# Leaf rows summed on VectorE instead of GpSimd, with another order of calls on every engine

## What is computed

```python
h = patches @ W.T + b                                        # tok
h = h + attn(layernorm(h))                                   # attn: x*res_scale + (u * (relu(qk/sqrt_s)^2 @ v)) @ o_w.T
logits = x @ W_in.T + b_in                                   # ffn, x = layernorm(h), 8 trees x 255 nodes
moves = logits > 0                                           # walk down: 7 decisions in each tree
out = (silu(logits) * visited) @ W_out.T                     # only the 8 nodes on the path are kept
h = h + out
```

## Time and profile before

| | |
|---|---|
| median of 3 runs | 2026.34 us (2025.54 to 2026.86) |
| profiled execution, own time | 2028.2 us |
| its span, first to last instruction | 2026.4 us |
| mean granted TensorE clock | 0.991 |
| PE busy | 1973.2 us, 97% |
| DVE busy | 1702.8 us, 84% |
| ACT busy | 1397.2 us, 69% |
| POOL busy | 1001.6 us, 49% |

### The profile page before, as it was taken

The page is one execution under the profiler, slowest core; times in us unless marked ns, Lnnn a source line. Parts: engine busy times, 40 slices in busy tenths (PEclk is TensorE's granted clock), DMA queues, the critical chain, the costliest instruction groups (busy, mean ns, idle before and its releaser), DMA issues. The chain is left out here.

```text
span 2026.4 us, 41146 instructions
## 1 busy us (share of the span) xinstructions
PE 1973.2 (97%) x12488; PEld 1858.1 (92%) x12488; DVE 1702.8 (84%) x4210; ACT 1397.2 (69%) x3085; POOL 1001.6 (49%) x1001
## 2 busy tenths in 40 slices
PE   6799999999999999999999999999999999999997
PEld 5689999999999999999999999999999999999986
DVE  5598888898888898888898888898888898888875
ACT  5467776677776676776676776676776776776764
POOL 2675445545445545445545545545545545545544
PEclk8999999999999999999999999999999999999999
DMA  4423223223222223223233223232223233222222
GB/s 131 108 75 93 76 77 82 79 72 90 77 75 81 78 76 87 74 77 80 75 83 84 75 76 82 73 86 83 75 75 81 74 87 83 75 75 79 61 68 80
DMA packets 81999, 163.12 MB, mean 80 GB/s; under 512 B 17102, under 2 KB 48048, under 8 KB 81968
## 3 DMA queue, kind: packets, MB, share of 16 engines
q0 software_dynamic: 40960, 103.02, 19.3%
q1 hardware_dynamic: 41008, 59.71, 10.3%
HBM read 148.76 MB, written 13.90 MB: 80 GB/s over the span
## 5 line engine op out<-in xcount | busy, mean ns | idle before, releaser
L483 POOL DMA_INDIRECT leaf_rows<-leaf_table,leaf_at x512 | 582.2, 1137 | 156.0 <-issue 156.0
L861 DVE TENSOR_TENSOR hid_lo<-hid,hid_hi 128x392 fp32r<-128x392 f32 (+1 forms) x256 | 255.3, 997 | 77.3 <-ACT hid_hi L551 77.2
L1168 PE MATMUL out_acc<-hid_hi,outw_lo 128*128 128x392 f32 x768 | 300.3, 391 | 0.2 <-DVE hid_lo L861 0.2
L456 POOL TENSOR_TENSOR inv_root<-to_root,minus_half 98x8 f32<-98x8 f32 x64 | 95.7, 1495 | 412.7 <-DVE to_root L911 266.1
L1168 PE MATMUL hid_ps<-ffn_x,in_lo 128*128 128x392 f32 x768 | 272.1, 354 | 1.8 <-ACT hid L706 0.7
L1170 PE MATMUL out_acc<-hid_hi,outw_hi 128*128 128x392 f32 x768 | 263.4, 343 | 0.0
L1169 PE MATMUL hid_ps<-ffn_x,in_hi 128*128 128x392 f32 x768 | 262.8, 342 | 0.0
L1169 PE MATMUL out_acc<-hid_lo,outw_hi 128*128 128x392 f32 x768 | 262.2, 341 | 0.0
L1170 PE MATMUL hid_ps<-ffn_x,in_hi 128*128 128x392 f32 x768 | 261.4, 340 | 0.0
L496 POOL TENSOR_TENSOR row_sum<-leaf_rows,row_sum 98x1024 f32<-98x1024 f32 x96 | 221.3, 2305 | 40.3 <-ACT leaf_rows L743 34.6
L482 POOL TENSOR_TENSOR held<-minus_half 98x1 f32<-98x1 f32 x128 | 35.7, 279 | 373.6 <-ACT v_full L637 199.6
(11 more groups left out here) (142 smaller groups left out, 5854.6 us busy)
## 6 DMA issues: line engine op xcount, KB each, us to landing
x_raw<-x SPq DMA_DIRECT2D x192, 196.0 KB, 2.4
out<-out_stage SPq DMA_DIRECT2D x32, 392.0 KB
leaf_rows<-leaf_table,leaf_at POOLq DMA_INDIRECT x512
leaf_table<-leaf_rows SPq DMA_DIRECT2D x4, 256.5 KB, 4.2
out_stage<-in_w SPq DMA_DIRECT2D x4, 256.0 KB
tok_major<-tok_w SPq DMA_DIRECT2D x3, 256.0 KB, 4.3
late_raw<-out_w SPq DMA_DIRECT2D x6, 128.0 KB
u<-uv_w SPq DMA_DIRECT2D x1, 576.0 KB, 4.2
```

Source lines behind the costliest of these rows:

```text
L483: pool.indirect_dma_start(row_slot(s, g), None, table, bass.IndirectOffsetOnAxis(ap=leaf_at[:, s, g:g + 1], axis=0), element_offset=s * P ...
L861: dve.tensor_tensor(out, src, hi.bitcast(F32), ALU.subtract).then_inc(done, 1)
L1168: pe.matmul(out, w[1], x_parts[0], start=start, stop=False)
```

## The change

`scale_rows` on ACT is left for the first tree only. For trees 1 to 3 a new `sum_rows` on DVE does scaling and adding in one instruction for each group of 98 tokens: row times activation (a scalar for each partition, read from `leaf_act`) plus sum. POOL's `sum_rows` goes. The counts that the fetches wait for follow. In addition every engine's table of calls is written in another order, and the cut between two trips lies elsewhere.

The hunks below are, in this order, the count of sums, POOL's `sum_rows`, ACT's `scale_rows`, DVE's new `sum_rows`, and the first calls of DVE's table.

```diff
-SUMS = GATHERED - 1
+SUMS = (GATHERED - 1) * GROUPS
...
-            def sum_rows(i, s):
...
-                pool.tensor_tensor(row_sum[:, :, :], leaf_rows[0:HALF, at:at + GROUPS, ROW_IN:ROW], row_sum[:, :, :],
-                                   ALU.add).then_inc(rows_summed, 1)
...
-            def scale_rows(i, s):
+            def scale_rows(i):
...
+            def sum_rows(i, s):
+
+                if i is None:
+                    return
+                dve.wait_ge(leaf_active, GATHERED * i + s + 1)
+                if s == 1:
+                    dve.wait_ge(rows_scaled, GROUPS * (i + 1))
+                for g in range(GROUPS):
+                    if s > 1:
+                        dve.wait_ge(rows_summed, SUMS * i + GROUPS * (s - 2) + g + 1)
+                    dve.scalar_tensor_tensor(row_sum[:, g], row_slot(s, g)[:, ROW_IN:ROW], leaf_act[:, s, g:g + 1],
+                                             row_sum[:, g], ALU.mult, ALU.add).then_inc(rows_summed, 1)
...
             def body(p, i, n, nx):
+                leaf_dots(p, 3)
+                x_low(n, 5)
+                sum_rows(p, 2)
+                sum_rows(p, 3)
+                hid_low(p, 6)
+                ffn_x_low(i, 0)
+                ffn_x_low(i, 1)
+                mask(p, 7)
                 norm_stats(n, 0, 0)
                 norm_stats(n, 0, 1)
                 norm_moments(n, 0)
                 decisions(i, 0)
```

More of the change, by code:

```diff
@@ L1080, in body @@
                 decisions(i, 0)
+                decisions(i, 1)
+                mask(i, 0)
                 hid_low(p, 7)
-                mask(i, 0)
-                decisions(i, 1)
                 hid_low(i, 0)
@@ L1091, in body @@
                 xn_low(n, 1)
+                mask(i, 2)
                 residual(n, 0)
@@ L1131, in body @@
                 mix_low(n, 3)
-                leaf_dots(i, 2)
+                hid_low(i, 5)
+                x_low(nx, 2)
                 mask(i, 6)
@@ L1135, in body @@
                 update_h(n, 1)
-                decisions(i, 7)
-                x_low(nx, 2)
+                leaf_dots(i, 2)
                 norm_stats(n, 1, 0)
                 norm_stats(n, 1, 1)
+                x_low(nx, 3)
                 norm_moments(n, 1)
-                x_low(nx, 3)
-                leaf_dots(i, 3)
+                decisions(i, 7)
                 x_low(nx, 4)
-                hid_low(i, 5)
-                x_low(nx, 5)
-                hid_low(i, 6)
-                ffn_x_low(n, 0)
-                ffn_x_low(n, 1)
-                mask(i, 7)
             dve.sem_inc(out_stored, 16)
@@ L1419, in body @@
             def body(p, i, n, nx):
+                turn_xn(i, 0)
+                turn_xn(i, 1)
+                tree_visits(p, 2)
+                tree_logits(p, 4, 0)
+                turn_normed(i, 0)
+                tree_out(p, 0, 0)
+                tree_out(p, 0, 1)
+                tree_visits(p, 3)
+                turn_normed(i, 1)
+                tree_out(p, 1, 0)
+                find_leaf(p, 2)
+                make_base(i)
+                tree_out(p, 1, 1)
+                if first(i):
+                    turn_rows()
+                make_v(i, 0)
+                tree_logits(p, 4, 1)
+                make_v(i, 1)
+                find_leaf(p, 3)
+                make_v(i, 2)
+                tree_logits(p, 5, 0)
+                make_v(i, 3)
+                tree_out(p, 2, 0)
+                tree_visits(p, 4)
+                tree_out(p, 2, 1)
                 make_u(i, 0)
[L1421 removed]
+                tree_out(p, 3, 0)
+                make_u(i, 1)
                 tree_logits(p, 5, 1)
                 scores(i, 0)
[L1424 removed]
+                scores(i, 1)
+                tree_out(p, 3, 1)
                 tree_logits(p, 6, 0)
[L1426 removed]
+                make_u(i, 2)
+                make_u(i, 3)
+                tree_logits(p, 6, 1)
+                mix(i, 0)
                 tree_visits(p, 5)
[L1428 to L1432 removed]
                 mix(i, 1)
                 mix(i, 2)
+                tree_out(p, 4, 0)
                 mix(i, 3)
                 tree_visits(p, 6)
[L1437 to L1438 removed]
+                tree_out(p, 4, 1)
                 project_o(i, 0, range(0, 3))
```

218 lines of the change are left out of this document (85 added, 133 removed).

## The result

The changed kernel takes 2035.21 us in the median of 6 runs (2032.7 to 2038.73), the kernel before 2026.44 us in 6 runs. The ratio is 1.0046 with a 95% interval of 1.0033 to 1.0059: slower by 0.46%, 8.8 us. The forecast was 2038 us, in a range of 2020 to 2048.

The account below looks back on a forecast made before the run. PE's own work was taken to bound the loop, with small waits tied to DVE. Loop +12.5, start +2.0 and end -2.7 us sum to +11.8 us on the median 2026.34, giving 2038 us, range 2020 to 2048.

Parts of the forecast that it names:

- tied DVE chain: DVE from `update_h(n, 1)` to the visit: 17.34 us behind `embed`; PE waits 0.80 us a period instead of 0.29.
- 29 periods: Loop between the first and 30th `add_rows`: +0.51 - 0.08 = +0.43 us a period, +12.5 us over 29.
- The new instruction: DVE's scale-and-add, 98 x 256: 0.345 us like a dot plus 0.05 to 0.06 for the scalar, taken as 0.40 us.
- not slower, about 2026: Rival: the new DVE instruction costs 0.345 us like a dot, so the period stays the old one; chance 0.16.
- The relief of DVE from POOL's addition: Long `hid_lo` in the tied stretch, held by POOL's addition, shortens; 2.0 us come back to DVE there.
- "wrong" sign: Profile sign against the forecast: a period of 60.9 us or less, or a PE wait elsewhere, above all at `turn_xn` or `mix`.
- The step saved on PE: `find_leaf(i, 1)` directly ahead of `turn_xn` saves one late second matmul, 0.08 us a period.
- The start: First unit: `norm_roots(0, 0)` starts at 24.7, 3.3 us later, and the unit hangs on it; +2 us, bounds -1 and +5.
- The end: Last unit: fetches and dot freed from POOL's addition 3.2 us earlier, eight sums added, `tree_out` of tree 5 earlier; -2.7 us.
- Faster, about 2015: Rival: DVE reaches the visit in time, chain 0.8 us shorter, both waits and one step go; chance 0.17.
- Slower still: Rival, about 2057 us: a new DVE instruction costs 0.48 us, 18.6 us more; chance 0.08.
- the relief fails: Rival, about 2096 us: a gather, not POOL's addition, held `hid_low`, which still takes 2.98 us; 58 us more; chance 0.02.

Follow-up runs that it names:

- experiment with a constant: Changed kernel, its 12 new DVE instructions using the constant 1.0 instead of the activation read for each partition; 2024.51 us, ratio 0.9995.
- experiment with the short addition: Kernel before, POOL's three additions cut to one column of each group; 2019.97 us, ratio 0.9971.
- version with the split sums: Changed kernel, tree 1's fetch no longer waiting for the next unit's first v, the last two of tree 3's four sums behind `decisions(i, 1)`; 2018.58 us.
- versions that move the sums of tree 3: Changed kernel, tree 3's four sums moved behind `decisions(i, 1)`: 2050.23 us; also without tree 1's fetch wait: 2041.28; only two sums moved, without that wait: 2018.58.
- Taking the hold away: Changed kernel, POOL's first gather of tree 1 no longer waiting for the next unit's first v; 2026.18 us, ratio 1.000.
- a start 5 us earlier: Version with the split sums, plus the first unit's last x piece split ahead of the v and u weights and `norm_roots(0, 0)` earlier on POOL; 2018.12 us.
- old tables with the sums replaced: Kernel before with its own tables, sums on DVE: tree 1 ahead of `gate(n, 0)`, tree 3 behind `decisions(i, 1)`, POOL's additions gone; 2034.73 us, ratio 1.0044.

## Why the prediction was right, step by step

The size and the sign were right, the mechanism in part. The period is longer by the tied DVE chain that the prediction named, and by a wait that it didn't have, and the second is the larger part: against the 0.29 us of before, the two places of the chain have 0.14 us more, and `mix` has 0.30. Of the three terms, the loop's came out near its size with this exchange inside, the end's was near, and the start's had the wrong sign. Start and end are read from one profiled execution of each kernel.

| term | predicted | measured (spans) |
|---|---|---|
| 29 periods | +12.5 us | +11.3 us |
| up to the first `add_rows` | +2 us | -1.9 us |
| from the 30th to the end | -2.7 us | -1.9 us |
| sum | +11.8 us | +7.5 us (medians +8.8) |

**The new instruction.** 0.40 us predicted, 0.396 measured, and the two parts that it was put together from (0.345 for the dot's shape, 0.05 to 0.06 for the scalar) came out as 0.336 and 0.060. The Trainium skill, page "VectorE: DVE Perf Modes", section on the TRN2 errata, has 58 + N cycles, an estimate of 0.33 us, and nothing for the scalar. The experiment with a constant agrees with it (0.336); with the activation the measurement decides. That was the step on which the sign hung: at 0.336 the kernel ties with the one before (2024.5 us), as the rival "not slower, about 2026" said. (The "about 2024" that the prediction has for 0.33 us is a slip: by its own terms, 8 x 0.07 us less in the chain, it comes to about 2022.)

**The relief of DVE from POOL's addition.** Right: no long `hid_lo`, 763 ns in the mean for 997, and the experiment with the short addition shows that it was the addition. The longest `hid_lo` of the loop is 2.99 us before, 0.97 after and 0.98 with the short addition. The Trainium skill, page "SBUF — State Buffer", section "Who interferes with whom", has an exclusive lock between such instructions; the traces agree. The experiment also showed what the prediction had only as an argument, that the hold cost the old loop next to nothing (60.93 us with and without).

**The tied chain.** Predicted 17.34 us from `embed` to the visit, measured 16.98. The steps between were 12.54 and came out as 12.26, and `mask` cost 0.95 instead of 1.03 (which was near its duration, 1.04, and not a distance between starts). The sums were 3.17 for 3.20; the rest is that `norm_stats` costs 1.34 us where the next instruction doesn't use its result (1055.02 to 1056.36), against the 1.46 that I took from a row where it does, and a few hundredths each in `ffn_x_low`, `hid_low` and the dots. So PE waits 0.43 us at the two places, not 0.80. This is the term that was mis-sized. Both waits are there, but of the second only 0.05 us depend on the chain: 0.13 to 0.16 us stay at the visit in every kernel in which `turn_h` doesn't wait for `ffn_x_low`, for there `norm_stats` waits for `turn_h` itself, and from `turn_h` to the visit it is 4.22 to 4.27 us by way of DVE. The prediction also took the old wait ahead of `turn_h(n, 0)`, 0.15 us, for one of the same kind. It wasn't. `ffn_x_low` had ended 0.98 us earlier, and ACT's `copy_h`, which writes what `turn_h` transposes, 0.05 us earlier, at 1060.18:

```profile
1059.11 1.07 ACT L574 ACTIVATE hT<-hid_ps,col 128x392 f32<-128x392 f32 x2
```

With ACT's new table `copy_h` ends 0.49 us ahead of `turn_h`. So "PE hardly waits for it, so I cost that at nothing" left out half of the old loop's waits: 0.15 us a period, 4 us in all, which the version with the split sums has back.

**The wait that I didn't see.** The "wrong" sign that I named for the profile, a wait at `mix`, is there, with 0.30 us; the other place named, `turn_xn`, has one in the versions that move the sums of tree 3. The new tables bring the dots of tree 1 nearer to its gathers. I had counted the calls around the tied stretch, not the distance from the held gathers to the dots: from the first gather's start on POOL to the first dot it was 1030.89 - 1020.06 = 10.8 us, and is 1031.87 - 1025.87 = 6.0 us. Taking the hold away gave 9.0 us back, as much as the whole slowdown; of the 9.6 us by spans, 8.5 lie in the 29 periods. That the period came out right (+0.43 predicted, +0.39 measured) is thus partly luck: 0.37 us too much in one place, 0.30 too little in another, and a step that wasn't saved.

**The step saved on PE.** -0.08 us a period, not seen. A usual period before was 60.93 us, less the waits 0.29 that is 60.64 of PE's own time; now it is 61.36 - 0.73 = 60.63, and in the version with the split sums 60.86 - 0.25 = 60.61. Where the new order of PE pays for what `find_leaf` saves wasn't tried.

**The start.** +2 us predicted, -1.9 measured. The sentence "the first unit hangs on it" failed. The root was later than I said (26.54 instead of 21.41; I said 24.7), because the last piece of `x` is now split behind the `v` and `u` weights, which I had overlooked. But none of it reaches the first `add_rows`: a start 5 us earlier gave nothing, as PE then waits for work that stands behind POOL's first gathers. Where the 1.9 us come from isn't shown. DVE without POOL's additions may be part of it (4.0 us in the experiment with the short addition, 2.0 in the old tables with the sums replaced), and the hold is another (the first `add_rows` stands at 149.4 without it). But two versions that differ in the order of tree 1's gathers alone have 149.4 and 152.0, so differences of this size are not to be built on.

**The end.** -2.7 predicted, -1.9 measured. The 8.51 us wait of the old kernel is gone; in its place the changed one has 2.07 us at the visit and 2.52 us at `tree_out` of tree 6, whose `hid_low` stands behind the eight sums, and 1.41 and 1.48 us ahead of them. That POOL's addition held the old end is borne out: without it, 2.8 us less; I had said 3.2.

**The rivals.** "Faster, about 2015" was judged possible if the chain were 0.8 us shorter. With the hold away and 0.8 us off the chain it is 2018.6. "Then both waits go" was wrong in it, since that at the visit stays. "Slower still" and "the relief fails" are out by the rows above.

## What to carry to other kernels

When work moves to an engine in a hand-ordered pipeline, the price of its instructions is easy to get within a few per cent from the nearest shapes. What it costs depends on where the calls stand: the same twelve instructions gave 2018.6, 2034.7 and 2149.7 us. Of each small wait of the engine that bounds the loop, find what ended it, by the ends of all that it could wait for: here one was put down to DVE and was ACT's. Go through every wait of the moved engine for what has come nearer to it, the DMAs and holds above all, and not only through the stretch in which the work was put. And before a call is moved, follow the buffer that it frees to the next writer; a wait of PE comes back as soon as one reader is later than that.

## What was not expected of the hardware

A scalar read for each partition costs DVE 0.060 us in each instruction of 98 x 256 (0.396 against 0.336 us from start to start). The hold of DVE by POOL's addition took 58 us of DVE's time in `hid_lo` alone (255.3 us busy against 197.1), and cost the loop some 1.4 us. Waits of PE can cost more than their length: with two of 1.0 us in a period, or one of 1.9, the granted clock was at half for 3.6 and 2.6 us of the period in the mean, another 1.8 and 1.3 us; with one of up to 1.2 us (the gathers reordered) it stayed at 1.00. And a mere reordering of four gathers on POOL's queue made DVE, ACT and PE stall for about a microsecond at another place of the period, while the same reordering with the gathers not held back and two of the sums elsewhere changed nothing; the traces don't show the cause.
